# A gated feed-forward block on one core: x in pairs of tiles from the start, w1 rounded two blocks at a time, intercepts on GpSimd, the last product in column halves, and new orders on every engine

## The reference, cut to what matters

```python
# x (4, 512, 512), ctx (4, 512, 128), w1 and w2 (1408, 512), w3 (512, 1408), all float32
x = x + tanh(g_xattn) * (0.6 * sigmoid(si[:, :, None] + sj[:, None, :] + b) + 0.4 * layernorm(x))
#   si, sj: ctx times the two halves of W (1, 256)
y = layernorm(x)
h = silu(bitlinear(y, w1)) * bitlinear(y, w2)
x = x + tanh(g_ffn) * bitlinear(h, w3)

def bitlinear(x, w):
    xn = x * rsqrt(mean(x * x) + 1e-6)
    xq = round(xn * 127 / max(abs(xn)))  (per row, and scaled back)
    wq = clip(round(w / mean(abs(w))), -1, 1)  (one scale for the whole matrix)
    return xq @ wq.T
```

## Time and profile before

| what | us |
|---|---|
| three runs | 155.89, 157.94, 158.43 (median 157.94) |
| the profiled execution | 157.06, its span 155.3, mean granted clock 0.978 |
| TensorE busy | 139.7 (90% of the span) |
| VectorE, ScalarE, GpSimd busy | 117.9, 107.3, 101.0 (76%, 69%, 65%) |
| chain that ended last | PE 72%, DVE 11%, DMA 5%, POOL 4% |

### The profile page before, as it was taken

One profiled execution on the slowest core, in us unless ns is written; L12 is line 12 of the kernel. 1 busy time (PEld: TensorE's weight loads), 2 busy tenths in 40 slices (PEclk: granted clock), 3 DMA queues, 4 the chain that ended last, 5 costly groups with the idle time before them and its releaser, 6 DMA issues.

```text
span 155.3 us, 2445 instructions
## 1 busy us (share of the span) xinstructions
PE 139.7 (90%) x743; PEld 76.7 (49%) x743; DVE 117.9 (76%) x180; ACT 107.3 (69%) x177; POOL 101.0 (65%) x155
## 2 busy tenths in 40 slices
PE   0984965798998999999999999999999999999991
PEld 0883854365555455444444444444454444454540
DVE  0338998998889999999979966489579184669441
ACT  3279998979598489967799286532999636772720
POOL 3302617999892791785989985669968999436210
PEclk9999599779999999999999999999999999999999
DMA  4899999999214189733193695453362807654313
GB/s 146 289 406 395 407 402 414 392 364 347 61 38 93 34 168 212 151 62 69 35 199 64 152 113 146 100 104 126 101 160 60 241 9 189 160 97 93 135 74 129
DMA packets 45237, 26.94 MB, mean 173 GB/s; under 512 B 35751, under 2 KB 37800, under 8 KB 45224
## 3 DMA queue, kind: packets, MB, share of 16 engines
q1 hardware_dynamic: 45216, 26.78, 60.9%
q10 hardware_dynamic: 8, 0.00, 0.0%
HBM read 13.89 MB, written 4.19 MB: 116 GB/s over the span
## 4 chain that ended last, share of the span: by engine, by line
PE 72%; DVE 11%; DMA 5%; POOL 4%; issue 3%; ACT 2%; SPq 1%; DVEq 0%; ACTq 0%; POOLq 0%
PE ps L1307 46%; PE ps L1341 24%; DMA raw_room<-in_L_ffn_w_dram 5%; DVE raw L1038 2%; DVE bn L922 2%; ACT w2T L656 1%; DVE w_abs L972 1%; POOL ln_r L440 1%; DVE w3q L1026 1%; DVE c_all L953 1%; DVE w1T L1009 1%; POOL raw L509 1%; DVE x_top L962 1%; PE ps L1290 1%; POOL slope L443 1%
## 5 line engine op out<-in xcount | busy, mean ns | idle before, releaser
L1307 PE MATMUL ps<-w1T,xqT 128*128 128x512 f16 (+1 forms) x192 | 42.3, 372 | 0.0
L1307 PE MATMUL ps<-w2T,xqT 128*128 128x512 f16 (+1 forms) x192 | 40.7, 361 | 1.1 <-ACT w2T L656 0.6
L1341 PE MATMUL ps<-w3T,hqT 128*128 128x512 f16 x176 | 40.1, 379 | 0.0
L1038 DVE SCALAR_TENSOR_TENSOR raw<-ps,deq,raw_room 128x1408 f32<-128x1408 f32 x16 | 26.9, 1683 | 16.6 <-PE ps L1307 11.2
L721 ACT ACTIVATE raw_room<-ps,deq 128x1408 f32<-128x1408 f32 x16 | 22.9, 1432 | 15.9 <-PE ps L1307 15.8
L521 POOL TENSOR_SCALAR hq<-raw,h_scale 128x1408 f16<-128x1408 f32 x15 | 23.8, 1590 | 9.9 <-DVE h_scale L1048 9.6
L1307 PEld LDWEIGHTS ps<-w1T,xqT 128*128 128x128 f16 x192 | 19.2, 100 | 20.6 <-issue 2.2
L1307 PEld LDWEIGHTS ps<-w2T,xqT 128*128 128x128 f16 x192 | 18.6, 98 | 20.9 <-DVE raw L1038 0.8
L1341 PEld LDWEIGHTS ps<-w3T,hqT 128*128 128x128 f16 x176 | 17.2, 98 | 19.3
L1045 DVE TENSOR_REDUCE h_top<-raw 128x1 f32<-128x1409 f32 x16 | 25.8, 1610 | 0.2
L732 ACT ACTIVATE junk<-raw 128x1410 f16<-128x1410 f32 x16 | 21.9, 1372 | 1.5 <-DVE raw L1038 1.3
(11 more groups left out here) (99 smaller groups left out, 173.5 us busy)
## 6 DMA issues: line engine op xcount, KB each, us to landing
c_all<-in_x_dram SPq DMA_DIRECT2D x16, 256.0 KB, 9.5
...
```

Of the source, the lines that this page charges most:

```text
L1038: v.scalar_tensor_tensor(out=hid[:, t % HS, 0:H], in0=ps_up[:, 0:H], scalar=deq[:, 1, t:t + 1], in1=gate[:, t % GATES, :], op0=ALU.mult, o ...
L1307: last = m.matmul(bank[:, lo:hi], xqT[:, i % XT, k, :], wT[w][:, k, lo:hi], start=(k == 0), stop=(k == KD - 1))
L1341: last = m.matmul(ps_y[t % 2], hqT[:, t % HT, k, :], w3T[:, :, k, :], start=(k == 0), stop=(k == KH - 1))
```

## The change

- UNITS begins with a pair: tiles 0 and 1 go through statistics, affine, make_x and max_x together. So UNITS has eight entries, not nine, and SGROUPS five.
- The affines are dealt out anew: ACT takes tiles 4, 5, 8 to 11, 14 and 15 (before 4 to 7, 10 and 11), DVE 12 and 13 as before.
- evac_rows takes two blocks of w1 in one instruction, out of two PSUM banks; there are six instead of eleven, five of them on ACT.
- Shares of the weights' sums move between ACT and DVE; all of w3 is summed by ACT.
- DVE converts four groups (of two blocks, the last of one) of w2 and one block of w3, POOL two groups and three blocks of w3 (before: DVE two groups, POOL four, and all four blocks of w3). DVE moves three transposed groups of w2 out of PSUM, ACT three (before two and four).
- intercept moves from DVE to POOL; ctx_out(2) from DVE to ACT.
- last_product(15) is two products of eleven matmuls with 256 columns, in two banks; finish(15) and store(15) follow in halves. The second half waits for finish(14), whose bank it takes.
- The lists of all five engines are new. gate_product(0) stands ahead of the transposes of w2, spread_scores(2) ahead of up_product(0), scores(3) behind up_product(3), last_product(0) behind up_product(4), square_h(15) behind evac_last. The loads at the head of SP's list stay.

```diff
-    UNITS = [(0, 1), (1, 2), (2, 4), (4, 6), (6, 8), (8, 10), (10, 12), (12, 14), (14, 16)]
+    UNITS = [(0, 2), (2, 4), (4, 6), (6, 8), (8, 10), (10, 12), (12, 14), (14, 16)]
-    SGROUPS = [(0, 1), (1, 2), (2, 4), (4, 8), (8, 12), (12, 16)]
+    SGROUPS = [(0, 2), (2, 4), (4, 8), (8, 12), (12, 16)]
-    AFFINE_ACT = [3, 4, 6]
-    AFFINE_DVE = [7]
+    AFFINE_ACT = [2, 4, 5, 7]
+    AFFINE_DVE = [6]
-    ABS_ACT = [[(0, 0, 3), (1, 5, 6), (2, 6, 8), (3, 10, 11)], [(1, 3, 6), (2, 6, 9), (3, 9, 11)], [(0, 0, 1), (1, 1, 2), (3, 3, 4)]]
-    ABS_DVE = [[(1, 3, 5), (2, 8, 9), (3, 9, 10)], [(0, 0, 3)], [(2, 2, 3)]]
+    ABS_ACT = [[(0, 0, 3), (2, 8, 9), (3, 9, 10)], [(1, 3, 6), (2, 6, 9)], [(0, 0, 1), (1, 1, 2), (2, 2, 3), (3, 3, 4)]]
+    ABS_DVE = [[(1, 3, 5), (1, 5, 6), (2, 6, 8), (3, 10, 11)], [(0, 0, 3), (3, 9, 11)], []]
-    CONV_DVE = [[], [0, 5], []]
-    CONV_POOL = [[], [1, 2, 3, 4], [0, 1, 2, 3]]
-    ROWS_ACT = [0, 4, 5, 8, 9]
-    ROWS_DVE = [1, 2, 3, 6, 7, 10]
+    CONV_DVE = [[], [0, 1, 2, 3], [2]]
+    CONV_POOL = [[], [4, 5], [0, 1, 3]]
+    ROWS_ACT = [0, 2, 3, 4, 5]
+    ROWS_DVE = [1]
-    OUT_DVE = [[], [0, 5]]
-    OUT_ACT = [[], [1, 2, 3, 4]]
+    OUT_DVE = [[], [0, 1, 2]]
+    OUT_ACT = [[], [3, 4, 5]]
...
+        def turned_rows(n):
+            lo, hi = 2 * n, min(2 * n + 2, KH)
+            bank = (lo % 6) * BANK
+            return (w1T[:, :, lo * P:hi * P].rearrange("p k (t c) -> p t k c", t=hi - lo),
+                    ps[:, bank:bank + (hi - lo) * BANK].rearrange("p (t k c) -> p t k c", t=hi - lo, k=KD), hi)
...
+        COLUMNS = [(0, D // 2), (D // 2, D)]
...
+            def intercept(u):            # on gpsimd; its twin on vector goes
+                lo, hi = UNITS[u]
+                if u == 0:
+                    pool.wait_ge(t_ready, 1)
+                pool.wait_ge(tanh_done, hi)
+                pool.wait_ge(slopes, SGROUP[hi - 1] + 1)
+                for i in range(lo, hi):
+                    ins = g.tensor_scalar(icept[:, i:i + 1], th_sum[:, i:i + 1], t03_neg[:, 0:1], slope_mean[:, i:i + 1],
+                                          ALU.mult, ALU.subtract)
+                ins.then_inc(icepts, 1)
...
gpsimd, the head of the new list:
+            slopes_x(0); intercept(0); affine_x(0); affine_x(1); quant_x(0); quant_x(1); slopes_x(1); intercept(1)
+            affine_x(2); affine_x(3); conv_w(1, 4); step_x(0); conv_w(1, 5); conv_w(2, 0); dequant_gate(0)
+            conv_w(2, 1); dequant_up(0); quant_x(2); hidden_floors(); quant_x(3); slopes_x(2); intercept(2)
+            conv_w(2, 3); step_x(1); dequant_x(1); intercept(3); quant_h(0); quant_x(4); affine_x(6); quant_x(5)
+            affine_x(7); mean_x(0); step_x(2); slopes_x(3); dequant_x(2); quant_h(1); dequant_h(0)
...
scalar:
+            ctx_out(0); gates(); sum_w(0, 0); score(0); sum_w(0, 1); score(1); sum_w(0, 2); score(2); score(3)
+            evac_rows(0); evac_rows(2); ctx_out(1); sum_w(1, 0); evac_rows(3); sum_w(1, 1); evac_rows(4); evac_rows(5)
+            evac_x(0); scores_out(1); square_x(0); sum_w(2, 0); sum_w(2, 1); sum_w(2, 2); evac_x(1); sum_w(2, 3)
+            square_x(1); ctx_out(2); evac_w(1, 3); evac_w(1, 4); evac_w(1, 5); scores_out(2); silu(0)
...
vector:
+            spread_out(); half_scores(0); sum_w(0, 0); sum_w(0, 1); gate_factors(); sum_w(0, 2); sum_w(0, 3)
+            stats_x(0); scale_w(0); evac_rows(1); clip_w1(0); sum_w(1, 0); make_x(0); half_scores(1); max_x(0)
+            clip_w1(1); stats_x(1); sum_w(1, 1); clip_w1(2); weight_factor(0); scale_w(1); conv_w(1, 0); conv_w(1, 1)
+            weight_factor(1); conv_w(1, 2); conv_w(1, 3); make_x(1); evac_w(1, 0); evac_w(1, 1); evac_w(1, 2)
+            scale_w(2); stats_x(2); half_scores(2); max_x(1); stats_x(3); clip_w3(0); hidden(0); max_h(0)
+            conv_w(2, 2); hidden(1); clip_w3(1); make_x(2); clip_w3(2); max_x(2); hidden(2); stats_x(4)
+            weight_factor(2); make_x(3); clip_w3(3); half_scores(3); hidden(3); stats_x(5); max_x(3); max_h(1)
+            stats_x(6); hidden(4); max_h(2); max_h(3); stats_x(7); max_h(4); hidden(5)
...
tensor:
+            turn_rows(0); spread_scores(0); turn_rows(1); turn_rows(2); sum_w(0); turn_rows(3 to 5); turn_ctx(1)
+            turn_rows(6); turn_rows(7); scores(1); turn_rows(8); turn_rows(9); spread_scores(1); turn_rows(10)
+            turn_x(0); sum_w(1); gate_product(0); turn_ctx(2); turn_x(1); turn_w(1, 0 to 3); sum_w(2)
+            turn_w(1, 4); scores(2); turn_w(1, 5); spread_scores(2); up_product(0); gate_product(1); up_product(1)
+            turn_ctx(3); gate_product(2); up_product(2); gate_product(3); up_product(3); scores(3); gate_product(4)
+            spread_scores(3); up_product(4); last_product(0); gate_product(5); up_product(5); last_product(1)
...
-                for k in range(KH):
-                    ...
-                    last = m.matmul(ps_y[t % 2], hqT[:, t % HT, k, :], w3T[:, :, k, :], start=(k == 0), stop=(k == KH - 1))
-                last.then_inc(y_ps, 1)
+                if t == T - 1:
+                    for n, (lo, hi) in enumerate(COLUMNS):
+                        if n == 1:
+                            pe.wait_ge(out_done[(T - 2) % OUTS], (T - 2) // OUTS + 1)
+                        for k in range(KH):
+                            ...
+                            last = m.matmul(ps_y[(t + n) % 2][:, 0:hi - lo], hqT[:, t % HT, k, :], w3T[:, lo // P:hi // P, k, :],
+                                            start=(k == 0), stop=(k == KH - 1))
+                        last.then_inc(y_ps, 1)
```

More of the change, by code:

```diff
@@ L555, in _ @@
+            step_x(0)
+            conv_w(1, 5)
+            conv_w(2, 0)
             dequant_gate(0)
+            conv_w(2, 1)
+            dequant_up(0)
+            quant_x(2)
+            hidden_floors()
+            quant_x(3)
+            slopes_x(2)
+            intercept(2)
+            conv_w(2, 3)
             step_x(1)
             dequant_x(1)
-            dequant_up(0)
-            hidden_floors()
+            intercept(3)
+            quant_h(0)
+            quant_x(4)
+            affine_x(6)
@@ L560, in _ @@
+            quant_x(5)
+            affine_x(7)
             mean_x(0)
-            conv_w(2, 0)
-            quant_x(2)
-            quant_x(3)
-            conv_w(2, 1)
+            step_x(2)
             slopes_x(3)
-            conv_w(2, 2)
-            step_x(2)
             dequant_x(2)
-            quant_x(4)
+            quant_h(1)
+            dequant_h(0)
+            quant_x(6)
             step_x(3)
+            mean_x(1)
+            quant_h(2)
             dequant_x(3)
-            quant_x(5)
@@ L594, in _ @@
-            quant_h(5)
-            dequant_x(5)
-            add_x(1)
-            dequant_h(2)
-            quant_h(6)
-            slopes_x(5)
-            add_x(2)
-            quant_x(10)
-            quant_h(7)
+            quant_x(7)
+            quant_h(3)
+            intercept(4)
+            quant_h(4)
+            dequant_h(1)
+            add_x(0)
+            intercept(5)
+            quant_h(5)
+            slopes_x(4)
+            quant_x(8)
+            step_x(4)
+            intercept(6)
@@ L603, in _ @@
+            add_x(1)
+            quant_x(9)
+            quant_h(6)
+            dequant_h(2)
+            mean_x(2)
+            quant_x(10)
+            dequant_x(4)
+            quant_h(7)
+            step_x(5)
             quant_x(11)
             quant_h(8)
+            intercept(7)
+            dequant_x(5)
+            mean_x(3)
+            quant_x(12)
+            dequant_h(3)
+            dequant_h(4)
+            quant_h(9)
+            add_x(4)
             step_x(6)
-            mean_x(3)
@@ L851, in _ @@
-            th_neg_x(3)
-            square_h(7)
+            finish(3)
+            silu(7)
+            square_x(10)
+            square_h(6)
+            score(14)
+            silu(8)
+            square_x(11)
+            score(15)
+            finish(4)
+            square_h(7)
+            th_neg_x(3)
+            square_h(8)
+            affine_x(14)
+            silu(9)
+            finish(5)
+            affine_x(15)
             finish(6)
+            square_h(9)
+            square_x(12)
@@ L1112, in _ @@
-            conv_w(1, 5)
-            stats_x(3)
-            scale_w(2)
-            weight_factor(1)
-            evac_w(1, 5)
-            weight_factor(2)
-            make_x(2)
-            half_scores(2)
-            max_x(2)
-            hidden(0)
-            stats_x(4)
-            max_h(0)
-            intercept(3)
-            clip_w3(0)
-            clip_w3(1)
-            hidden(1)
+            clip_w1(1)
+            stats_x(1)
+            sum_w(1, 1)
+            clip_w1(2)
+            weight_factor(0)
@@ new lines, in _ @@
+            scale_w(1)
+            conv_w(1, 0)
+            conv_w(1, 1)
+            weight_factor(1)
+            conv_w(1, 2)
+            conv_w(1, 3)
+            make_x(1)
+            evac_w(1, 0)
```

(13 more changed lines are left out.)

388 lines of the change are left out of this document (159 added, 229 removed).

## The result

| kernel | runs, us | median | ratio to before |
|---|---|---|---|
| before | 155.89, 157.94, 158.43, 157.20 | 157.57 | |
| changed | 161.13, 161.62, 161.83, 161.66 | 161.64 | 1.029 [1.020, 1.038] |

The changed kernel is slower, by 4.1 us of the median. I had said 156.8 and 154.7 to 159.6; the time lies above the range. The profiled execution took 161.13, its span 159.3 (before 155.3), mean clock 0.957. The other three of the changed kernel had a mean clock of 0.967 to 0.968 and took 161.62 to 161.83 all the same. So they may have lost less to the clock than the profiled one and more elsewhere; what follows is told of the profiled one.

What follows compares the result with a forecast made beforehand. TensorE's nearly unbroken stream of products was taken to bound the kernel. On the profiled 157.06 us, +0.15 for the stream's end and -0.55 for the tail gave 156.65; it predicted 156.8, range 154.7 to 159.6.

Steps and rivals of the forecast that it cites:

- free: Intercepts on GpSimd: eight pairs, 4 us, in an engine 65% busy, said to cost nothing where it waits for VectorE anyway.
- 0.7 for new small waits: Stream of products: new waits put at 0.7 us, the size of the old ones that go.
- both slower rivals: Head slips, up_product(0) at 38.4 and slow clock, 159.5 us, chance 0.23; stream stalls, 158.4 us, chance 0.17.
- the second ending after 29.5: Head, VectorE's conversions: a sign deciding for the rival that the head slips, span 157.7, chance 0.23.
- my "against": Argument against the head slipping: consecutive VectorE clips kept GpSimd out instead, and TensorE had held clock 1.00 despite gaps.
- slopes_x(3) and hidden(4): Stalling stream rival: chain with 0.6 us of slack, two or three waits of 0.5 to 1 us, chance 0.17.
- up_product(0) at 37.3: End of the head: up_product(0) starts at 37.3 us, bounds 36.5 and 38.4, 0.6 later than before.
- A pair of intercepts 0.5, bounds 0.4 and 1.5: GpSimd: us per pair, from smallest operations of 0.24 to 0.3; a step beside a VectorE multiply-add took 1.30.
- it lands near 59.7: SP's queue: the last turn of w3, behind turn_h(0), lands near 59.7 us, for last_product(0) at 60.5.
- 0.5 to 1.9 of slack at each product: Stream from tile 6 on: slack in us found at each product.
- The tail: Behind the last product: -0.55 us, from -0.26 for the last VectorE step and -0.3 for the halved store.
- by that the store would give nothing: Last store: under about 2 us fixed DMA cost, halving gains nothing and the tail is 0.3 poorer.

Runs made afterwards that it cites:

- a3: Changed kernel with spread_scores(2) back behind up_product(0) and scores_out(2) behind th_neg_x(0); 162.24 us, ratio 1.032.
- a2: Changed kernel with GpSimd holding conv_w(1, 4) back until VectorE's make_x(1) is done; 160.84 us, ratio 1.017.
- d1: c1 with the intercepts back on VectorE; 159.10 us, ratio 1.013.
- c1: a2 and a6 together on the changed kernel, plus 14 dummy matmuls of 192 columns behind turn_w(1, 2); 157.97 us, ratio 1.000.
- b1: Kernel before with the intercepts moved to GpSimd and nothing else; 160.86 us, ratio 1.020.
- a6: Changed kernel with turn_w3(2) ahead of turn_x(4), dequant_x(5) ahead of intercept(7), affine_x(14) behind silu(9); 158.95 us, ratio 1.010.
- a7: Changed kernel with make_x(1) moved behind half_scores(2) in VectorE's list; 160.24 us, ratio 1.012.
- c2: c1 with 24 more dummy matmuls of 128 columns behind turn_x(0); 157.73 us, ratio 1.003.
- d3: Kernel before with the last product in column halves and, on VectorE, clip_w3(0) and clip_w3(1) ahead of intercept(3); 156.75 us, ratio 0.994.
- d2: c2 with 22 dummy matmuls instead of 14 behind turn_w(1, 2), and 8 more ahead of scores(2); 157.00 us, ratio 1.001.

## Why the prediction was wrong

- **The step that failed.** My sum put the meeting of VectorE and GpSimd, and what queues behind it, at nothing: the intercepts "free", make_x(1) 1.2 us long, "0.7 for new small waits". It gave a span of 154.9, and 159.3 was measured. Of the 4.4 between, up_product(0) makes 1.48 (38.78 for 37.3), its clock 1.48, waits 1.57 (2.27 for 0.7) and the tail -0.18.
- **The range.** I had both slower rivals, and together my figures give 154.9 + 1.1 + 1.7 + 1.7 = 159.4 for the span. I gave the two together 0.08 and left them out of the range, which ended with one of them at 159.6. That the figures fit so well is in part luck, for the places were others. I had VectorE's conversions held up by GpSimd, with the second ending after 29.5 as the sign; it ended at 29.11 and GpSimd was the one shut out, as my "against" had it. The other sign, up_product(0) over 3 us, came. For the stream I named slopes_x(3) and hidden(4); silu(4) came 25.3 us after the stream's start (my sign was 25.2), and no product waited for it. The waits came at last_product(0) and gate_product(10).
- **up_product(0) at 37.3.** It came at 38.78, although the first rounding was 0.3 sooner than I had it (15.98). Of the 1.83 that the head is longer than before, 0.25 is spread_scores(2) (a3; I had 0.44), 0.80 is make_x(1) (a2), and 0.71 the intercepts on GpSimd (d1 against c1), by a way that is not shown. Each is the difference of two executions. The pairs of x and the new shares of the sums, by which w2's scale comes 11.6 us after w1's and not 9.4, were never undone by themselves, so what they cost the head is not measured. I had make_x(1) at 31.5 and 1.2 long; it was 31.88 and 2.38.
- **A pair of intercepts 0.5, bounds 0.4 and 1.5; "free", slack of 1 us.** Bare it is 0.73; held up it took up to 3.08, beyond my upper bound. I bounded it with a wait for one multiply-add, but VectorE runs four conversions without a gap, and the second column got in now after two of them (1.91), now only after the last (3.08, c1). The slack did not exist (b1: 3 us), for an intercept in the list also waits for ScalarE's tanh.
- **Stream: 0.7 of waits.** It was 2.27. The new SP order was the one that I called harmless ("it lands near 59.7"). But 59.7 is near the time at which the last transpose of w3 is issued (59.35 before, 59.94 now), and the 3.5 us or more that it takes to land have no place in it. It stands behind turn_x(4), and a6, which takes one transpose out from behind that, issues it at 57.55. The second wait came from an affine in ScalarE's list ahead of silu(9), in a part where I claimed "0.5 to 1.9 of slack at each product". And the wait of 0.27 before 63.25 that I read in the trace of before is not there: the product there starts 0.05 late.
- **The clock of up_product(0)** was in the rival, not in the forecast. It fell in 5 of the 17 profiled executions: after, a3, a7, c2, d3; four of the eleven with the new lists, one of the six with the old. So part of the 1.48 is the execution's luck. Whether the changed kernel is more exposed to it stays open.
- **Right:** gate_product(0) at 26.8 for 26.2, at the slow level, without use (d2 shows that it would not have been of use at the full level either); the scale of w2 at 27.56 for 27.05; ScalarE's pair 1.02 from start to start and 1.11 long; the pair on VectorE 1.28 in place of 1.25; evictions and half_scores(2) ending together; square_h(15) free.
- **The tail:** -0.73 for -0.55. The last VectorE step gave 0.27 of it. From that step's end to the end of the span it took 2.10 (before 2.48): half the bytes gave 0.38, for a store of 256 KB cut to 128. The Trainium skill, "DMA: Bandwidth & Descriptors", section "Latency and other measured facts", speaks of a fixed cost of about 2 us. It doesn't say there that the bytes cost nothing, so my "by that the store would give nothing" did not follow from it, and the 0.38 does not speak against it.
